# Merged TensorE signals, a copy moved on ScalarE, and later steps for indirect transfers in a vision tower of attention and routed experts

## What is computed

```python
h = tok(x)                            # 8x8 patches @ W + b + pos_embed: 16 x 1024 tokens x 64
xi = layernorm(h).reshape(n, 64, 1024)
K, Q, V = Wk @ xi + bk, Wq @ xi + bq, Wv @ xi + bv
K = softmax(K over tokens); Q = softmax(Q over the 8 channels of a head)
h = h + (Wr @ (ctx(K, V) applied to Q) + br + xi).T
z = layernorm(h)
probs = softmax(z @ gate_w + gate_b); top two, renormalised
h = h + sum over the two experts e of  p_e * ((silu(z @ w1[e]) * (z @ w2[e])) @ w3[e])
```

## Time and profile before

| | |
|---|---|
| median of 3 runs | 795.47 us (794.19 to 797.77) |
| profiled execution, its own time | 794.0 us |
| its span, first to last instruction | 792.1 us |
| mean granted TensorE clock | 0.86 of full |
| busy, share of span | PE 73%, GpSimd 65%, DVE 56%, ACT 44% |
| indirect transfers | 256 scatters, 255.2 us busy; 256 gathers, 244.3 us busy |

### The profile page before, as it was taken

How to read it: one execution, slowest core, us unless ns; L and a number is a source line. 1 busy time by engine, 2 the same in 40 slices (tenths; PEclk the granted TensorE clock), 3 DMA queues, 4 the chain that set the end, 5 groups by cost and what they waited for, 6 DMA issues and landing times.

```text
span 792.1 us, 14179 instructions
## 1 busy us (share of the span) xinstructions
PE 577.0 (73%) x3844; PEld 479.5 (61%) x3844; DVE 443.1 (56%) x1237; ACT 347.6 (44%) x753; POOL 518.1 (65%) x540
## 2 busy tenths in 40 slices
PE   5867668787899989898889988998959702973000
PEld 3455536585688668867786778686848702873000
DVE  5655653656556776776667567756755601454111
ACT  2233122152546466646564666456626701674111
POOL 2051077366771777777777777777777777777774
PEclk9987875597999999999999899989969965997555
DMA  2599032233463375528442844374344414544121
GB/s 78 111 243 388 1 96 82 71 106 94 129 186 84 78 177 146 150 54 199 135 136 55 201 128 122 75 180 115 107 117 128 113 51 123 139 101 98 40 40 30
DMA packets 168871, 93.20 MB, mean 118 GB/s; under 512 B 99680, under 2 KB 152928, under 8 KB 168800
## 3 DMA queue, kind: packets, MB, share of 16 engines
q1 hardware_dynamic: 151632, 66.71, 32.0%
q0 software_dynamic: 16384, 25.20, 11.7%
q10 hardware_dynamic: 784, 0.39, 0.2%
HBM read 45.06 MB, written 47.19 MB: 116 GB/s over the span
## 4 chain that ended last, share of the span: by engine, by line
PE 33%; POOL 26%; DVE 16%; issue 13%; DMA 6%; ACT 4%; POOLq 0%; ACTq 0%; DVEq 0%; SPq 0%
POOL sums L504 13%; POOL rows_scratch L487 9%; PE wide_ps L1013 6%; PE h_ps L1145 4%; PE y_ps L1162 3%; DMA hx<-xi_scratch 3%; DMA xi_scratch<-xi 2%; POOL hx L504 2%; POOL kexp L504 2%; PE turn_ps L1129 2%; DVE twice_y L953 2%; PE wide_ps L1105 2%; PE wide_ps L1033 2%; PE hidT_ps L1155 1%; PE wide_ps L1019 1%
## 5 line engine op out<-in xcount | busy, mean ns | idle before, releaser
L487 POOL DMA_INDIRECT rows_scratch<-z_parts,place x256 | 255.2, 997 | 128.7 <-issue 77.5
L504 POOL DMA_INDIRECT sums<-y_scratch,place x224 | 213.9, 955 | 83.6 <-issue 67.1
L1145 PE MATMUL h_ps<-w_hi,rowsT 128*128 x384 | 112.6, 323 | 39.3 <-DVE hid_all L955 34.0
L953 DVE SCALAR_TENSOR_TENSOR twice_y<-tanh,h_ps 128x256 f32<-128x256 f32 x192 | 79.6, 414 | 108.0 <-ACT tanh L601 90.1
L1145 PEld LDWEIGHTS h_ps<-w_hi,rowsT 128*128 128x128 f32 x384 | 75.5, 197 | 53.8 <-issue 52.4
L1162 PE MATMUL y_ps<-w_sb,hidT_all 128*128 x768 | 102.6, 279 | 1.0 <-ACT twice_y L614 1.0
L1145 PE MATMUL h_ps<-w_lo,rowsT 128*128 x384 | 101.5, 291 | 0.0
L1162 PEld LDWEIGHTS y_ps<-w_sb,hidT_all 128*128 128x128 f32 x768 | 99.1, 202 | 2.1 <-issue 2.1
L601 ACT ACTIVATE tanh<-h_ps 128x256 f32<-128x256 f32 x192 | 69.8, 386 | 63.7 <-PE h_ps L1145 58.5
L1129 PE MATMUL turn_ps<-ident,rows_all 128*128 128x128 f32 x384 | 62.5, 288 | 47.7 <-DMA rows_all<-rows_scratch 40.8
L955 DVE SCALAR_TENSOR_TENSOR hid_all<-twice_y,h_ps 128x256 f32<-128x256 f32 x192 | 80.7, 420 | 6.6
(11 more groups left out here) (250 smaller groups left out, 907.1 us busy)
## 6 DMA issues: line engine op xcount, KB each, us to landing
rows_all<-rows_scratch SPq DMA_DIRECT2D x96, 256.0 KB
y_scratch<-twice_y SPq DMA_DIRECT2D x96, 128.0 KB
rows_scratch<-tanh SPq DMA_DIRECT2D x3, 3072.0 KB, 19.5
xi_scratch<-xi SPq DMA_DIRECT2D x16, 256.0 KB, 3.4
rows_scratch<-z_parts,place POOLq DMA_INDIRECT x256
hx<-xi_scratch SPq DMA_DIRECT2D x14, 256.0 KB
sums<-y_scratch,place POOLq DMA_INDIRECT x224
out<-sums SPq DMA_DIRECT2D x56, 64.0 KB
```

Of the source, the lines that this page charges most:

```text
L487: gp.indirect_dma_start(rows_dram[n], bass.IndirectOffsetOnAxis(ap=place[m % RING][:, r, j:j + 1], axis=0), z_parts[m % 2][:, j // 2, j % ...
L504: gp.indirect_dma_start(y_of[r][apart(m)][:, j // 2, j % 2, :], None, y_dram[m % 3], bass.IndirectOffsetOnAxis(ap=place[m % RING][:, r, j: ...
L953: ve.scalar_tensor_tensor(twice[:, j, :], tanh[:, j, :], 1.0, halves[:, j, 0, :], ALU.add, ALU.mult).then_inc(S["twice_done"], 1)
L1145: mm = te.matmul(h_ps[:, j * 256:(j + 1) * 256], rowsT[g % 2][:, j * P:(j + 1) * P], w[:, bass.ds(experts[g][j], 1), :, :].rearrange("d a ...
```

## The change

Three edits are made together.

1. TensorE's three signals become one, step_done, which is raised once at the end of each step's project_out. Who waited for one of the three now waits for a count of step_done: for a turn the step in which it is made (rows_turned), for turn_hidden the step after its group's (inner_turned), for project_out two after (projected). For pairs 3 to 7 the two signals of the embedding, the pairs of signals of the four q/v blocks and the three of the attended result are raised together at the last of them.
2. ScalarE copies hidT one step later, and at another place: `copy_hidT(g-2)` stands between `turn(g+1)` and `copy_y(g-3)`.
3. The steps of the indirect transfers: scatters from the fifth pair on begin two steps later, gathers one or two steps later from the second to the seventh pair, and both spread over six and a half steps in place of six (2 or 3 columns a step).

```diff
-SCATTER = (16, 22, 28, 44, 57, 70, 83, 96)
-GATHER = (38, 50, 63, 76, 89, 102, 110, 122)
+EVEN, GROUPS_NEXT = 4, 13
+SCATTER = (16, 22, 28, 44, 59, 72, 85, 98)
+GATHER = (38, 51, 65, 78, 91, 104, 111, 122)
...
+        def rows_turned(groups):
+            return groups
+        def inner_turned(groups):
+            return groups + 3 if groups > 0 else 0
+        def projected(groups):
+            return groups + 4 if groups > 0 else 0
...
-                        if first[m] + j * SPREAD // COLS == s:
+                        if SCATTER[m] + (j * SPREAD // COLS if m < EVEN else j * GROUPS_NEXT // (2 * COLS)) == s:
...
+                        if GATHER[m] + (j * SPREAD // COLS if m == 0 else (COLS + j * GROUPS_NEXT) // (2 * COLS)) == s:
...
-                    wait(pool, "rowsT_ps_ready", min(s - LAG + 2, GROUPS_ALL))
+                    wait(pool, "step_done", rows_turned(min(s - LAG + 2, GROUPS_ALL)))
...
             def turn(g):
-                wait(act, "rowsT_ps_ready", g + 1)
+                wait(act, "step_done", rows_turned(g + 1))
...
             def copy_hidT(g):
-                wait(act, "hidT_ps_ready", g + 1)
+                wait(act, "step_done", inner_turned(g + 1))
...
-                wait(act, "y_done", g - 1)
+                wait(act, "step_done", projected(g - 1))
...
                     turn(g + 1)
+                if 0 <= g - 2 < GROUPS_ALL:
+                    copy_hidT(g - 2)
                 if 0 <= g - 3 < GROUPS_ALL:
                     copy_y(g - 3)
                 for m, k in steps_at(s):
                     attend(m, k)
                 if 0 <= g < GROUPS_ALL:
                     activate(g)
-                if 0 <= g - 1 < GROUPS_ALL:
-                    copy_hidT(g - 1)
...
-                mm.then_inc(S["qv_ps_ready"], 1)
+                if m < 3:
+                    mm.then_inc(S["qv_ps_ready"], 1)
+                elif r % 2 == 1:
+                    mm.then_inc(S["qv_ps_ready"], 2)
...
-                        mm.then_inc(S["att_ps_ready"], 1)
+                        if m < 3:
+                            mm.then_inc(S["att_ps_ready"], 1)
+                    if m >= 3:
+                        mm.then_inc(S["att_ps_ready"], 3)
...
                 if 0 <= g + 2 < GROUPS_ALL:
-                    turn(g + 2)
+                    mm = turn(g + 2)
                 if 0 <= g - 2 < GROUPS_ALL:
-                    project_out(g - 2)
+                    mm = project_out(g - 2)
+                if 0 <= g + 2 < GROUPS_ALL + 4:
+                    mm.then_inc(S["step_done"], 1)
```

More of the change, by code:

```diff
@@ L266, in vit_kernel @@
             past_ready owner_ps_ready owner_ready ranked place_summed place_ready
-            rowsT_ps_ready rowsT_ready h_done tanh_done twice_done hid_done hidT_ps_ready hidT_ready y_done y_ready
+            step_done rowsT_ready h_done tanh_done twice_done hid_done hidT_ready y_ready
             part_ready gated_ready result_ready""".split()
@@ L351, in load_rows @@
                 wait_on(sp, scattered[m % 3], 16 * 2 * COLS * (m // 3 + 1))
-                wait(sp, "rowsT_ps_ready", g - 2)
+                wait(sp, "step_done", rows_turned(g - 2))
                 if g == 0:
@@ L482, in scatter @@
                     if m >= 3:
-                        wait(pool, "rowsT_ps_ready", GROUPS * (m - 2))
+                        wait(pool, "step_done", rows_turned(GROUPS * (m - 2)))
                     else:
@@ L505, in gather, with scatters_at, gathers_at @@
                                           bass.IndirectOffsetOnAxis(ap=place[m % RING][:, r, j:j + 1], axis=0)).then_inc(gathered[apart(m)][q], 16)
-            def columns_at(s, first):
+            def scatters_at(s):
                 for m in range(PAIRS):
                     for j in range(COLS):
-                        if first[m] + j * SPREAD // COLS == s:
+                        if SCATTER[m] + (j * SPREAD // COLS if m < EVEN else j * GROUPS_NEXT // (2 * COLS)) == s:
+                            yield m, j
+            def gathers_at(s):
+                for m in range(PAIRS):
+                    for j in range(COLS):
+                        if GATHER[m] + (j * SPREAD // COLS if m == 0 else (COLS + j * GROUPS_NEXT) // (2 * COLS)) == s:
                             yield m, j
@@ L516, in _ @@
                 if 0 <= s - LAG < GROUPS_ALL:
-                    wait(pool, "rowsT_ps_ready", min(s - LAG + 2, GROUPS_ALL))
-                for m, j in columns_at(s, SCATTER):
+                    wait(pool, "step_done", rows_turned(min(s - LAG + 2, GROUPS_ALL)))
+                for m, j in scatters_at(s):
                     scatter(m, j)
-                for m, j in columns_at(s, GATHER):
+                for m, j in gathers_at(s):
                     gather(m, j)
@@ L604, in copy_hidT @@
             def copy_hidT(g):
-                wait(act, "hidT_ps_ready", g + 1)
+                wait(act, "step_done", inner_turned(g + 1))
                 if g == 0:
                     act.wait_ge(S["h2_ready"], 3 * 2)
-                wait(act, "y_done", g - 1)
+                wait(act, "step_done", projected(g - 1))
                 sc.activation(hidT[g % 2][:, :], hidT_ps[:, :], ACT.Copy).then_inc(S["hidT_ready"], 1)
             def copy_y(g):
-                wait(act, "y_done", g + 1)
+                wait(act, "step_done", projected(g + 1))
                 wait_on(act, y_stored[g % 2], 16 * (g // 2))
@@ L948, in multiply @@
                 halves = h_ps[:, :].rearrange("p (j n h) -> p j n h", j=GROUP, n=2)
-                wait(dve, "hidT_ps_ready", g - 1)
+                wait(dve, "step_done", inner_turned(g - 1))
                 for i, j in enumerate(HALVES):
@@ L1018, in embed @@
                     for b in range(2):
-                        te.matmul(wide_ps[:, b * 512:(b + 1) * 512], ident[:, :], pos_in[:, :, :].rearrange("p t e -> p (t e)"),
-                                  start=False, stop=True).then_inc(S["emb_ps_ready"], 1)
+                        mm = te.matmul(wide_ps[:, b * 512:(b + 1) * 512], ident[:, :], pos_in[:, :, :].rearrange("p t e -> p (t e)"),
+                                       start=False, stop=True)
+                        if m < 3:
+                            mm.then_inc(S["emb_ps_ready"], 1)
+                    if m >= 3:
+                        mm.then_inc(S["emb_ps_ready"], 2)
             def queries(m, r):
```

7 lines of the change are left out of this document (4 added, 3 removed).

## The result

The changed kernel takes 855.56 us (median of 4 runs, 851.34 to 857.75) beside 794.83 us for the kernel before: a ratio of 1.075, 95% interval 1.070 to 1.081. The forecast was 831 us, 804 to 846. The sign and the mechanism were right and the size was not: the time lies above the range. The profiled execution has a span of 854.1 us, 62.0 more than before.

A forecast was written before the change was run, and what follows sets the result against it. GpSimd's gapless run of 416 transfers was taken as the bound. TensorE's delays of 8 us in front and 39 us over four periods, less 10.6 us cover, gave 36.4 us on 794.0: 830.4, stated as 831 us, range 804 to 846.

The forecast's parts named there:

- less 10.6 us: Seventh scatter: permission lets it end at 572.4, it ended at 583.0, so 10.6 us of TensorE's lateness is covered.
- at seven tenths from the seventh slice to the last: GpSimd's profile slices before the change: no other engine is busy to the end, so GpSimd is the suspected bound.
- 9.7 us forecast: TensorE's 13-step period: delays from hidT's copy and merged signals sum to 9.7 us, bounds 3 and 13.
- 4.4 for steps 73 to 75: q blocks and vals copies: turn_hidden waits for ScalarE, 3.0 us at step 73 plus 1.4 by step 75's qturn.
- +1.3: Step 66: z_parts, then rowsT and hidT copies on ScalarE delay turn_hidden from 415.77 to 417.1, 1.3 us.
- The rows of 71 and 77: Step 71: kexp starts later, +1.1 us; step 77: VectorE's adds await all three parts, turn_hidden +1.8 us.
- The forecast's 3.0 for this one step: Step 73: both q blocks wait for one signal, vals and weighing copies follow, the turn comes at 465.8, +3.0 us.
- "+0.6" at step 67: Step 67: squares waits for both embedding halves, VectorE's chain to xi and hid_all comes 0.6 us late, TensorE waits.
- 8 + 39 = 47: TensorE's lateness by step 88: 8 us before step 38 (bounds 3 and 10), 39 us from four periods after it.
- the weights of TensorE's work come at the low clock more often once it idles more: Rival of a much slower kernel, by this or by steps 73 to 75 losing all: 846 to 860 us, chance 0.08.
- The 0.8 us at the first gather: First gather waits for y_ps' end, 253.54, in place of the turn's end near 252.7: +0.8 us, nothing hides it.
- Worth 0 at best: Later steps for GpSimd's transfers: a saturated engine gains nothing from later permission; the cost is cover.

The follow-up runs named there:

- filled_three: Changed kernel plus unread TensorE matmuls at three places of pairs 3 to 7: six before turn_hidden in two steps, two more at step 66; 835.35 us, ratio 1.053.
- qv_att: Kernel before with only the q/v blocks' signals merged in twos and the attended result's three merged into one, pairs 3 to 7; 795.36 us, ratio 1.002.
- filled: Changed kernel plus six unread 128x256 matmuls on TensorE before turn_hidden in each of two steps of pairs 3 to 7; 840.53 us, ratio 1.056.
- move_only: Kernel before with only the copy of hidT moved a step later, ahead of the y copy, all signals apart; 810.96 us, ratio 1.020.
- parts_apart: Changed kernel with the signals of embedding, q/v blocks and attended result apart again, as before; 829.51 us, ratio 1.042.
- filled_two: Same kernel as filled, run once more on the chip of filled_three; 842.89 us, ratio 1.062.
- step_signal: Changed kernel with hidT's copy back on its own signal and the signals inside a pair apart; one turn/projection signal and new tables stay; 795.64 us, ratio 1.002.

## Why the prediction was right, and where it was off

**The bound and its cover: right.** The seventh scatter's end was said to move by TensorE's lateness at step 88 less 10.6 us. TensorE was 70.2 late, which gives 59.6, and the fifth gather starts at 643.89 for 583.00, 60.9 later. From there nothing was to be added, and the last transfer is 62.0 later. The kernel's time is GpSimd's run, and TensorE acts on it only through permissions. One reading was loose: "at seven tenths from the seventh slice to the last" passes over a 3, two sixes and a 1 in slices 8 to 13; the row without a dip starts at slice 14, behind the first gather, and it is there that the bound holds.

**The order on ScalarE as the cause: right.** TensorE's idle before hidT_ps was to grow to 20 us or more, most in the steps of vals; it grew to 62.4, 37 us of it in the two steps of the vals copies.

**The period: the step that failed.** By groups of steps, in us late on TensorE, from the ends of project_out:

| steps | forecast | after, three pairs | filled_three | qv_att |
|---|---|---|---|---|
| 65 to 68 | 2.4 | 6.3, 3.5, 3.3 | 1.5, 1.8, 4.3 | 0.3, 0.3, 0.3 |
| 69, 70 | 0 | 0.3, -0.5, 1.8 | 0.2, 0.6, 2.0 | 1.1, 1.0, 1.4 |
| 71, 72 | 1.1 | 0.9, 0.8, 0.9 | 0.9, 0.9, 0.9 | 0 |
| 73 to 76 | 4.4 | 8.0, 6.5, 7.8 | 4.7, 5.1, 3.5 | 1.2, 1.5, 1.2 |
| 77 | 1.8 | 1.8, 1.8, 1.8 | 1.8, 1.9, 1.8 | 0.9, 0.9, 1.0 |
| sum | 9.7 | 17.3, 12.1, 15.7 | 9.2, 10.2, 12.6 | 3.5, 3.7, 3.9 |

The term of the sum that was mis-sized is the period: 9.7 us forecast, 15.0 measured on the mean. Two rows carry the surplus: steps 73 to 75, "4.4 for steps 73 to 75", and the first steps of the period, "+1.3" at step 66. The rows of 71 and 77 came within 0.3 us. In both that failed the sum took the work behind a longer wait at the durations that TensorE has when it seldom waits. Step 73 shows it to the tenth: from turn_hidden to project_out TensorE needs 3.58 us (512.94 to 516.52) where it needed 2.98 with 0.82 of them idle, 2.16 of work. That is 1.42 more. The forecast's 3.0 for this one step and 1.4 are the 4.4 us that it lost; in filled_three, at a granted clock of 1.00 in this step, it lost 2.8. Step 66 lost 6.0, 3.1 and 3.0 us, and 1.2 to 1.6 in filled_three. Smaller terms did not come: "+0.6" at step 67 and 0.5 at step 65 were 0.0 and -0.1, with 0.5 at step 68 that the forecast did not have.

Together with the front (11.7 for 8) the period makes TensorE 70.2 us late at step 88, where the forecast had 8 + 39 = 47. These 23 us are the distance from 831 to 855.56, but for 1.4.

Where TensorE is kept busy the mean of the three sums is 10.7, close to the forecast's 9.7, and the time is 835 us beside the forecast's 831. Part of that closeness is luck, since filled_three still has stretches at the low clock. Its 4.3 us in steps 65 to 68 of one pair are one: 2.2 of them stand in step 65, for which the forecast had 0.5, behind idle times of 1.65 and 0.61 us. There the row of project_out and the window of the step are:

```profile
442.94 1.81 PE L1203 MATMUL y_ps<-w_sb,hidT_all 128*128 x8
```

```profile
438.76:444.75 5.99, 5.38 (x25) 5.39 (x26) 4.61 (x16) 2.56 (x6) 4.46 (x6) 0.50 0.36 109
```

The same project_out takes 1.00 us at full clock.

The prediction names this as its last rival, "the weights of TensorE's work come at the low clock more often once it idles more", and prices it at 846 to 860 with a chance of 0.08. It worked out new idle times in two steps of each period and the matmuls behind them, and priced these matmuls at full clock. The other price stood in the trace of the kernel before, in the front, where the same blocks ran in a window (150 to 156 us) with a granted clock of 0.50:

```profile
148.41 1.91 PE L1033 MATMUL wide_ps<-proj_qv,hx 128*128 128x256 f32 x4
...
151.92 3.79 PE L1059 MATMUL side_ps<-kT,vals 128*128 128x128 f32 x16 [1.35 <-ACT vals L563]
```

These are the 1.91 and, nearly, the 3.62 us of the changed kernel.

**The front.** 8 us were forecast up to step 37, with a bound of 10, and it was 11.7. Steps 34 and 35, the same q/v blocks of the pair in front, lost 9.0 us there, 5.8 in filled, and 4.1 in move_only and parts_apart, so both the clock and the merged signals have a part in it. The whole miss of 3.7 us is no more than the 4.5 us by which the first gathers of filled and filled_two, one kernel, differ.

**Signals.** The 0.8 us at the first gather held (0.5 in step_signal). That fewer signals give TensorE nothing held too. The Trainium skill's page "TensorE: Matmul & The Clock Gate" (The cost: per-tile semaphore tail) counts a cost for an increment on every matmul; no more than 0.2 us over 13 steps is seen here for one per block of four or eight. The merged signals inside a pair were forecast as parts of other terms, some 2 us together; qv_att shows 2.1 in their own steps. The 1 to 1.4 more at the load of the normed rows, which the prediction does not have, stand at a granted clock of 0.74 to 0.88.

**The tables.** "Worth 0 at best" and a loss of cover: 0.999 alone, 18 us in the changed kernel.

**What stays open.** Why the clock falls behind one idle time and not behind another of the same length, and from one execution to the next. And how the 41 us that fillers do not give back divide between the idle times themselves and the low clock that is left.

## What to carry to other kernels

A wait that is made longer on TensorE has two prices: its own length, and the work behind it at half the clock. The second can be as large as the first: at step 66 an idle time of 1.16 us came with a loss of 3.0 us, where the same step lost 1.2 to 1.6 with the clock kept up. A steady part at full clock does not show it before the change, but a stretch at the low clock elsewhere in the same trace gives the durations to reckon with. Where one engine is the bound and another has slack, list the slack first: here each of three edits alone (the first in its two halves) costs 0 to 2%, and together 7.5%, since they draw on the same cover. Before moving a copy to save a stop, follow what stands ahead of it at its new place in the steps that are full, not in the usual ones.

## What the hardware showed

The lower clock stood behind short idle times of TensorE: 1.16 us at 459.74, then the patch matmuls in 3.31 us; 1.22 us in filled_two, then 0.68 of the clock. It did not come every time: behind 3.63 us the clock was back by the next project_out (1.00 us at 516.52), behind 4.57 us it stayed low through the context matmuls (x16), and in one pair of the changed kernel the patch matmuls were at 1.99 us. The Trainium skill's page "TensorE: Matmul & The Clock Gate" (HAM oscillation — how this bites in real kernels) describes a kernel that waits between bursts and has its clock put back each time; this trace agrees that the clock falls behind waits, with 0.73 for 1.00. It differs in two things: the fall did not come each time, and it came behind waits of 1.2 us, where the page's are about 3 to 5 us. Two matmuls of 128x256 in place of a part of such a wait kept the clock up for the patch matmuls in all four pairs. Work that nobody reads made the kernel 13 to 20 us faster than the changed one, though not faster than the kernel before.
